# The second tile's closing sum on VectorE, moved behind the next pair's second sum of squares

## The reference

```
q = _rope(_rms(x @ Wq.T, q_norm_scale), pos)      # 8 heads of 32
k = _rope(_rms(x @ Wk.T, k_norm_scale), pos)      # 4 heads of 32
v = x @ Wv.T
_rms(x)  = x * rsqrt(mean(x*x) + EPS) * (1 + scale)
_rope(x) = concat([x1*cos - x2*sin, x2*cos + x1*sin])
k_blocks, v_blocks: the new k and v rows are written at (block, offset), then read back
p = softmax(q k^T * SCALE within a window of 128 positions), o = p v, out = o @ Wo.T
```

## Time and profile before

| what | value |
|---|---|
| median of 3 runs | 496.12 us (494.07 to 496.88) |
| the profiled execution: its own time | 497.69 us |
| its span in the trace | 495.9 us |
| TensorE busy | 382.6 us (77%) |
| VectorE busy | 345.0 us (70%) |
| ScalarE busy | 266.1 us (54%) |
| GpSimd busy | 107.7 us (22%) |

### The profile page before, as it was taken

The page is one execution under the profiler, slowest core; times in us unless marked ns, Lnnn a source line. Parts: engine busy times, 40 slices in busy tenths (PEclk is TensorE's granted clock), DMA queues, the critical chain, the costliest instruction groups (busy, mean ns, idle before and its releaser), DMA issues.

```text
span 495.9 us, 16985 instructions
## 1 busy us (share of the span) xinstructions
PE 382.6 (77%) x6190; PEld 283.8 (57%) x6190; DVE 345.0 (70%) x1017; ACT 266.1 (54%) x977; POOL 107.7 (22%) x178
## 2 busy tenths in 40 slices
PE   1753777888875006969879999999899999987996
PEld 0342534444442004757767777777777777776785
DVE  6994277898889805647656677677777777765782
ACT  3302555666665105545645766666766676654662
POOL 5300043333334620211211221211211221220000
PEclk9855798999999555799989999999999999998999
DMA  3999122222212066788877768867878969875200
GB/s 111 386 399 385 44 79 74 73 78 72 78 55 81 21 140 169 154 163 172 191 191 168 163 169 171 169 153 165 186 173 160 191 173 162 180 188 128 71 24 23
DMA packets 68866, 73.57 MB, mean 148 GB/s; under 512 B 18190, under 2 KB 65326, under 8 KB 66528
## 3 DMA queue, kind: packets, MB, share of 16 engines
q1 hardware_dynamic: 61968, 39.38, 33.9%
q0 software_dynamic: 6864, 33.72, 25.0%
HBM read 70.83 MB, written 26.21 MB: 196 GB/s over the span
## 4 chain that ended last, share of the span: by engine, by line
PE 32%; DMA 18%; ACT 9%; issue 5%; DVE 1%; SPq 1%; ACTq 0%; DVEq 0%; POOLq 0%
PE probT_bank L1123 6%; ACT rope L608 6%; PE out_bank L1147 5%; DMA kvbuf<-new_scratch,winidx 5%; PE score_banks L1084 4%; PE keys_bank L1066 3%; DMA window<-value_scratch 3%; DMA value_scratch<-kvbuf 3%; PE score_banks L1079 3%; ACT window L599 3%; PE out_bank L1134 3%; DMA out<-early 3%; DMA kvbuf<-in_kv,winidx 2%; PE out_bank L1148 2%; PE out_bank L1141 2%
## 5 line engine op out<-in xcount | busy, mean ns | idle before, releaser
L608 ACT ACTIVATE rope<-score_banks,negm 128x176 f32<-128x176 f32 x256 | 102.0, 414 | 4.2 <-DVE negm L886 4.0
L886 DVE TENSOR_REDUCE negm<-score_banks 128x2 f32<-128x352 f32 x128 | 61.0, 518 | 35.1 <-PE score_banks L1084 34.4
L896 DVE TENSOR_SCALAR rope<-rope,rinv 128x176 f32<-128x176 f32 x256 | 69.6, 314 | 4.6
L624 ACT COPY early<-probT_bank 128x128 f32<-128x128 f32 x64 | 17.0, 266 | 88.4 <-PE probT_bank L1123 88.4
L1011 PE MATMUL probT_bank<-wts,x2T 128*128 128x512 f32 x128 | 63.1, 617 | 1.8 <-DVE early L732 1.8
L433 POOL DMA_INDIRECT new_scratch<-stage,rowidx x32 | 36.5, 1142 | 111.9 <-DVE stage L757 107.0
L903 DVE COPY rope<-probT_bank 128x512 f32<-128x512 f32 x64 | 44.3, 692 | 18.6 <-PE probT_bank L1103 14.9
L608 ACT ACTIVATION_READ_ACCUMULATOR rope<-score_banks,negm 128x1 f32 x256 | 54.3, 212 | 0.0
L1123 PE MATMUL probT_bank<-rope,window 128*32 128x64 f32 x2048 | 43.8, 226 | 6.3 <-issue 3.4
L599 ACT COPY window<-keys_bank 128x352 f32<-128x352 f32 x60 | 46.7, 779 | 1.5 <-PE keys_bank L1066 1.5
L1066 PE MATMUL keys_bank<-ident,kvbuf 88*128 88x88 f32 x240 | 32.8, 262 | 16.0 <-ACT window L599 13.9
(11 more groups left out here) (179 smaller groups left out, 705.4 us busy)
## 6 DMA issues: line engine op xcount, KB each, us to landing
value_scratch<-kvbuf SPq DMA_DIRECT2D x16, 704.0 KB
window<-value_scratch SPq DMA_DIRECT2D x16, 512.0 KB, 11.6
work<-in_x SPq DMA_DIRECT2D x16, 256.0 KB, 2.7
new_scratch<-window SPq DMA_DIRECT2D x2, 2048.0 KB, 12.0
out<-early SPq DMA_DIRECT2D x32, 128.0 KB, 5.8
window<-value_scratch SPq DMA_DIRECT2D x32, 96.0 KB, 8.6
new_scratch<-kvbuf SPq DMA_DIRECT2D x1, 2048.0 KB, 14.2
wts<-in_weights SPq DMA_DIRECT2D x1, 1280.0 KB, 8.2
```

What stands on the lines that cost most here:

```text
L608: ins = a.activation(prob[:, par, P_AT[h]:P_AT[h] + KEYS], psS[:, h, 0:KEYS], ACT.Exp, bias=negm[:, par, h:h + 1], accum_out=sums[:, par, ...
L886: v.tensor_reduce(negm[:, par, 2 * half:2 * half + 2], psS[:, 2 * half:2 * half + 2, 0:KEYS], axis=AX_X, op=ALU.max, negate=True).then_inc ...
L896: ins = v.tensor_scalar(prob[:, par, at], prob[:, par, at], rinv[:, par, h:h + 1], None, ALU.mult)
```

## The change

In VectorE's `part2` the two closing sums of a pair stood one behind the other, between the sum of squares and the product of the following pair's first tile. Now the second stands behind the sum of squares of the following pair's second tile:

```
                 if s2:
                     sumsq(i * 2 + 2, 0)
                 if s3:
-                    for j in range(2):
-                        finish(i * 2 + j, j, i)
+                    finish(i * 2, 0, i)
                 if s2:
                     norm(i * 2 + 2, 0)
                     sumsq(i * 2 + 3, 1)
+                if s3:
+                    finish(i * 2 + 1, 1, i)
+                if s2:
                     norm(i * 2 + 3, 1)
```

## The result

The changed kernel takes 501.72 us in the median of 15 runs, the kernel before 496.12. The ratio is 1.0102, with a 95% interval of 1.006 to 1.0144: slower by 5.1 us (3.0 to 7.1).

A forecast was written before the change was run, and what follows sets the result against it. A ring of waits through four engines, 6.31 us a turn, was taken as the bound; 4.2 + 1.35 - 0.4 = +5.15 us on the profiled 497.69 gives 502.84, which lies 1.57 above the median, so 501.3; range 498.0 to 505.0.

The forecast's parts named there:

- What bounds the kernel: Query and key stage: no engine is full; a chain of waits through four engines sets the turn, 6.31 us.
- the ring: One turn's waits: sum of squares, first closing sum, both scatters, landing, value row, square; 6.29 us, the whole turn.
- The moved sum: VectorE: the second closing sum, moved behind reciprocal, product and sum of squares, ends at 139.66 instead of 138.47.
- The second scatter: GpSimd, each turn: prepared only after its release, it starts 0.37 us later; bounds 0 and 0.46.
- One sign that I named: GpSimd: the second scatter's idle time would be put down to VectorE's stage sum, no longer to issue.
- the first rival: GpSimd: preparation is hidden and the second scatter starts when it did; 496.1 us, no change; chance 0.12.
- Company: Second scatter starting together with the next rotations loses 0.05 us a turn; bounds 0 and 0.16.
- The fourth rival: VectorE holds up the second scatter by one rotation of some 0.4 us per turn; 5.6 more, 506.9 us; chance 0.04.
- Turns: Query and key stage: ten turns lose 4.2 us, the four before them 1.35 (bounds 0 and 2.5).
- The end of the stage: Last turn: VectorE's rotations, closing sums and masks come earlier and the last scatter follows; -0.4 us, bounds -0.45 and 0.
- VectorE does not set the turn: Denies the rival that VectorE, 90% busy, is the bound and closes a 0.37 us gap per turn; 490.9 us; chance 0.05.
- The third rival: TensorE's clock falls as its idle gap grows from 1.27 to 1.7 us; 5.6 more, 506.9 us; chance 0.05.

The follow-up runs named there:

- e3: Changed kernel with ScalarE's second value row of a pair moved from ahead of the first square to behind the first root; ratio 1.0022 to the kernel before.
- e4: Kernel before with ScalarE's second value row of a pair moved from ahead of the first square to behind the first root; ratio 0.99.
- e1: Changed kernel with the second closing sum one place earlier, ahead of the second sum of squares; median 502.01 us of 4 runs, beside 496.65 before.
- e8: Kernel before with one unused two-input VectorE addition more per turn, running as the first scatter starts; one run, 499.37 us.
- e9: Changed kernel with the second early gather moved behind the fifteenth pair's two scatters; one run, 497.67 us.
- e2_last: Changed kernel with the second closing sum two places later, behind the second tile's product, and one wait more; ratio 1.0691 to the kernel before.
- e7: Kernel before with the second value row behind the first root on ScalarE and the masks built before the stage; ratio 0.9872.
- e6: Changed kernel with the attention masks built before the query and key stage; median 495.42 us of 4 runs, beside 500.14 of the kernel before.

## Why the prediction was right

The forecast of 501.3 us (measured 501.72) followed the path that the traces show; its terms were not all of the right size, and that it came within half a microsecond is partly luck, as the sum below shows.

- *What bounds the kernel.* Right. e3 and e4 take the landing out of the ring, and the change's price goes from 0.36 to 0.06 us a turn.
- *The moved sum.* The closing sum was put 2.13 us behind the turn's start and ran at 135.99 - 133.86 = 2.13.
- *The second scatter.* Put at 3.45 behind the turn's start; ran at 137.31 - 133.86 = 3.45. The preparation is not hidden: from the end of the closing sum to the scatter's start it is 0.77 (137.31 - 136.54), as for the first scatter, and the 0.67 of the earlier trace rows came back as 0.68. One sign that I named was wrong: the idle time is still put down to "issue", not to VectorE, since the release at 136.54 falls into the first scatter's run. The Trainium skill (DMA: Bandwidth & Descriptors, "Anatomy of one DMA — SWDGE (gpsimd) path") gives some 50 ns for the sequencer's dispatch and calls the descriptor generation behind it small. No run splits the two; between release and start the trace has 0.77 us, more than tenfold, and the first rival, which leaned on that figure, fell.
- *Company.* 0.05 a turn was too much: between 93 and 159 us all twenty scatters took 0.982 to 0.985, although the second starts together with a rotation. Company does cost, in another place than I looked: 0.30 when the addition is running already as the scatter starts (e1, e8). The Trainium skill (GPSIMD Engine Reference, "1. Specifications") names contention with VectorE's instructions with two SBUF inputs. The traces agree as far as such an instruction is already running. The fourth rival's mechanism exists, but in the changed kernel it meets no regular turn: in these the rotation starts with the scatter (both at 137.31 in the turn above). It meets three scatters outside the ten turns, at 67.77, 76.21 and 164.00, which took 1.19, 1.15 and 1.15; this is the second, with the rotation that began 0.13 us ahead of it:

```profile
76.08 0.61 DVE L740 TENSOR_TENSOR early<-early,rope 128x256 f32<-128x256 f32 x2
76.21 1.15 POOL L433 DMA_INDIRECT new_scratch<-stage,rowidx  x1 [0.60 <-issue]
```

- *Turns.* Ten turns lost 3.58 (4.2 forecast), the four early ones 0.77 (1.35 forecast).
- *The end of the stage.* The term that missed: -0.4 forecast, -0.09 measured. VectorE is earlier, but the last pair's first closing sum waits 0.41 us for a landing that stands behind the early gather. I had named this as the bound ("a landing may hold it") and taken the other end; e9 gives most of it back.
- *The sum.* Forecast +5.15; the terms measured in the trace give 3.58 + 0.77 - 0.09 = 4.26, which would be 500.4 and not 501.72. The medians differ by 5.60, the ratio gives 5.1 (3.0 to 7.1), and both fit 4.26 as well as 5.15: the nearness of forecast and median lies within the spread of the runs, and is no evidence for the extra.
- *The other rivals.* VectorE does not set the turn: it now stands 0.93 us in each. TensorE's gap grew to 1.62 (135.72) against 1.27, and the clock stayed at its upper level, 1.00 in the ten turns. The third rival's fall of the clock does occur in e2_last: TensorE stood 4.39 us before 113.47, and the clock granted over the turn from 111.62 to 119.52 was 0.78.

## What to carry to other kernels

Follow one turn of a loop through all the engines and add it up: when the pieces give the whole turn, everything on that ring costs in full, however idle its engine is. An instruction that only releases others should stand as early as what waits for it needs, and an indirect transfer needs it some time before the engine comes free, not at that moment: here by 0.77 - 0.30 = 0.47 us, an estimate from the two distances in the list below, since no run places a release near that edge. To get such a loop faster, take a wait off the ring (here one value row, moved behind the root) before shortening an engine's queue. And look at what runs beside a transfer as it starts: moving the masks away from the last scatter gave 4.85 us (e7), about as much as the change cost (4.57 in the trace).

## What the runs showed of the hardware

- A scatter starts 0.77 to 0.78 us behind the end of the closing sum that releases it, or 0.30 to 0.31 behind the scatter ahead of it, whichever is later. That holds in each of the ten regular turns of all ten traces: 0.77 of a long idle GpSimd in e2, 0.77 in the changed kernel, where the release came 0.09 us before the first scatter ended (0.68 of idle engine), 0.30 behind the first scatter where the release came early (before, e1, e4, e7, e8).
- A scatter takes 0.98 us, but 1.28 with an addition of 0.55 us, both inputs in SBUF, that began 0.12 or 0.13 us ahead of it (e1, e8). The same sum, begun 0.34 us behind the scatter's start (135.99 against 135.65), a sum of squares with one input running as it starts, or a product with one of its two inputs in PSUM costs nothing.
- What is lost goes with what is left of such an instruction as the scatter starts: 0.42 left and 0.30 lost (e1), 0.28 left of the rotation's first part of 0.42 and 0.16 lost (1.15 against 0.98, changed kernel at 76.21), 0.10 left and nothing lost (e2, second scatters of the regular turns). Three points show the trend, not the rule.
- Beside the masks, VectorE instructions of 4.42 and 2.34 us, the last scatter took 5.80 us, and 0.98 without them (e6).
